# A four-layer graph network on one core: the second pair of squared edge components, read from memory instead of made by TensorE

## The chip, the core and the metric
The kernel runs on one core of a Trainium2 chip. The metric is the device time of one execution in microseconds. Five engines work on separate instruction streams and meet through semaphores: PE (TensorE, matmuls into the accumulator banks), DVE (VectorE), ACT (ScalarE), POOL (GpSimd) and SP (SyncE, which issues DMAs).

## The reference, cut to what matters
The reference runs four graph layers over 3125 nodes with 64 features and 103125 edges that are sorted by destination. The second layer is the one that the change touches. For each edge it forms, in the logits:

```python
h   = gelu(gelu(edge_attr_64 @ Wk1) @ Wk2)          # 64 hidden numbers of an edge
k   = f(h @ Wk3)                                    # times x[src], and times edge_sh (8 components)
q   = node_feat[edge_dst]
scal = concat([q * k0, einsum('ed,eds,es->ed', q, k1, edge_sh)])
edge_logit = scal @ W_logit                         # 4 heads
```

`k1` already holds one factor `edge_sh[s]`, so the sum over the eight components carries each component squared. The kernel therefore needs, for every edge, the product of a hidden number with the square of component s, for s = 0 to 7, before a matmul with the part of `Wk3` that belongs to s.

## The kernel before, in words
The first and the last two layers work on a dense count matrix and lie outside the change. Between them stand two edge passes over 202 tiles (`T`) of 512 edges (`TW`); the change is in the first, which makes the logits.

In the first pass edges lie along the free dimension of most tiles. Two components go into one 128-partition tile: component 2j on partitions 0 to 63 and 2j+1 on 64 to 127, each repeated over its 64 partitions. Pairs j = 0, 1 are the first pair of products (`bt_pair[0]`), j = 2, 3 the second (`bt_pair[1]`).

The squares are made for 16 tiles at a time (`CT`; 13 groups, `CN`): VectorE's `split_step` squares the raw components (L1697), and cuts each square into three bf16 parts, which SP stores as 24 rows to `sh_rows` (L533). For each tile SP loads these rows twice (`p1_components`, L569). TensorE's `tb(t, j)` (L925) is a matmul of a 0/1 selection matrix with these rows: it adds the three parts and repeats a component over 64 partitions, into banks 5 and 6. VectorE's `times(t, i)` (L1751) multiplies both banks by the hidden tile `h2k` into `bt_pair[i]`. As there are two banks only, the order is: `tb` 0 and 1, `times` 0, `tb` 2 and 3, `times` 1, and then `tb` 0 and 1 of the next tile. TensorE's `kmm` (L931) multiplies each result by its weights.

Every engine's order is written out by hand. One turn of TensorE's loop (L993) holds: the hidden layer of tile t+1 (L949), the first `tb` pair of t-1, the second hidden layer of t (L939, L940), `kmm` 2 and 3 of t-2, the logits of t-3 (L959), a fold every fourth tile (L968), the transposes of t (L975), the second `tb` pair of t-1, the node's own part of t-1 (`p1_half`, L983, which waits for the product of the tile before), and `kmm` 0 and 1 of t-1. One turn of VectorE (`p1`) holds: `times` 0 of t-1, one step of filling in destination rows (`fill`, L1738), the product of t-2 with its node features (L1762), a `fill`, `times` 1 of t-1, two `fill`, and `both` (L1745, source times destination features of t+1, which raises `u_ready`); in 9 of 16 turns a `split_step` follows.

SP's turn (`p1_turn`) issues the store of gathered rows (`xs_dump`, L573), waits for `u_ready` (L1745) and then issues the loads of placed rows (L565) and edge attributes (L562) two tiles ahead, the component rows of t (L569), and the store of the value hidden tile (`hs_dump`, L578). GpSimd gathers source rows, four indirect DMAs a tile (L734): the first waits for `xs_dump` of the tile two before and for `u_ready`, the second for a `times` 0, the third for a product, the fourth for a `times` 1.

Of the kernel before, what the change touches and what calls it, by code (L numbers as in the profile page):

```python
# [16 lines left out]
P = 128  # L17
N, D, E = 3125, 64, 103125
# [5 lines left out]
TW = K * P  # L24
S = 8
CT = P // S
CN = -(-T // CT)
# [16 lines left out]
COLS = 512  # L44
# [18 lines left out]
class Steps:  # L63
# [5 lines left out]
    def ran(self, ins):  # L69
        ins.then_inc(self.sem, 1)  # L70
        self.n += 1
# [23 lines left out]
def build(nc, x_in, src_in, dst_in, dst_before, dst_after, ea64, ea8, ew, w0, a0, gam, bet, wk1, wk2, wk3, wv1, wv2, wv3,  # L95
          wlog, wout, w2, a2s, a2d, b2, aw3, const, out):
    F32, BF16, F16, I32 = mybir.dt.float32, mybir.dt.bfloat16, mybir.dt.float16, mybir.dt.int32
    ALU, ACT, AX = mybir.AluOpType, mybir.ActivationFunctionType, mybir.AxisListType.X
# [10 lines left out]
    placed_v = placed[0:P * W, :].rearrange("(p c) f -> p (c f)", p=P)  # L109
    xs_dump = nc.dram_tensor("xs_dump", (P, W * D), F32).ap()  # L110
    sh_rows = nc.dram_tensor("sh_rows", (2, CN, 3 * S, CT * TW), BF16).ap()
    hs_dump = nc.dram_tensor("hs_dump", (T, D, TW), F32).ap()
    run_rows = nc.dram_tensor("run_rows", (P * W, D), F32).ap()
    carry_rows = nc.dram_tensor("carry_rows", (HROWS, D), F32).ap()
# [2 lines left out]
    with ExitStack() as ctx:  # L117
# [3 lines left out]
        def sem(name):  # L121
            return ctx.enter_context(nc.semaphore(name))
# [128 lines left out]
        def stage():  # L251
            c = Carve()
            c.at = stage_at
            return c

        cw = stage()
        wk3n, wv3n = cw(9 * D), cw(9 * D)
        eat = [cw(TW // 2) for _ in range(2)]
        sht = [cw(TW, BF16) for _ in range(2)]
        ut = [cw(TW // 2) for _ in range(2)]  # L260
        h1 = [cw(TW) for _ in range(2)]
        lgt = cw(P)
# [2 lines left out]
        bt_pair = [cw(2 * TW) for _ in range(2)]  # L265
# [6 lines left out]
        raw, square = ([cw(TW) for _ in range(2)] for _ in range(2))  # L272
# [29 lines left out]
        banks = ctx.enter_context(nc.psum_tensor("banks", [P, 8 * COLS], F32))  # L302
# [44 lines left out]
        hs_out = [sem(f"hs_out{i}") for i in range(2)]  # L347
        u_ready, ut_ps, ut_sb = sem("u_ready"), sem("ut_ps"), sem("ut_sb")
        sht_in = [sem(f"sht_in{i}") for i in range(2)]
        h1_ps, h1_sb, h2_ps, h2k_sb, h2v_sb = (  # L350
            sem("h1_ps"), sem("h1_sb"), sem("h2_ps"), sem("h2k_sb"), sem("h2v_sb"))
        tb_ps, bt_sb, half_k, yk_ps, prod_sb, lg_ps, lg_sb = (
            sem("tb_ps"), sem("bt_sb"), sem("half_k"), sem("yk_ps"), sem("prod_sb"), sem("lg_ps"), sem("lg_sb"))
# [25 lines left out]
        def at(sem_, value, eng):  # L379

            if not (isinstance(value, int) and value <= 0):
                eng.wait_ge(sem_, value)
# [29 lines left out]
        def _(sp):  # L412
# [51 lines left out]
            for i in range(SL // 8):  # L464
# [3 lines left out]
                if lo < W * D:  # L468
                    n = min(CROW, W * D - lo)
# [59 lines left out]
            def store_components(c):  # L529
                sp.wait_ge(split_sb, c + 1)  # L530
                for v in range(2):
                    for k in range(3):
                        sp.dma_start(sh_rows[v, c, k * S:(k + 1) * S, :].rearrange("s (g n) -> (s g) n", g=CT),  # L533
                                     parts[v][k][c % 2]).then_inc(split_out[c % 2], 16)

            def components_stored(c):
                sp.wait_ge(split_out[c % 2], 16 * 6 * (c // 2 + 1))

            sp.wait_ge(p_ready, NB)
            sp.wait_ge(agg_ps, 4)  # L540
# [3 lines left out]
            for k in range(2):  # L544
                r = slice(k * D, (k + 1) * D)
# [11 lines left out]
            for s_ in range(S):  # L557
                half = s_ % 2
# [8 lines left out]
            def p1_components(t, par):  # L567
                for k in range(2):
                    sp.dma_start(sht[par][D * k:D * k + 3 * S, :], sh_rows[0, t // CT, :, t % CT * TW:(t % CT + 1) * TW]).then_inc(sht_in[par], 16)  # L569

            def p1_rows(t, par, n):
                sp.wait_ge(gathered[par], n)
                sp.dma_start(xs_dump[:, bass.ds(t * (K * D), K * D)], xs[par]).then_inc(xs_out[par], 16)  # L573
# [7 lines left out]
            def p1_turn(t, par, n, more=True):  # L581
                p1_rows(t, par, n)
                if more:
                    sp.wait_ge(u_ready, t + 1)
                    p1_first(t + 2, par)
                    sp.wait_ge(h1_ps, t + 1)
                    p1_load(t + 2, par)
                if t > 1:
                    sp.wait_ge(tb_ps, t * 2 - 2)
                    p1_components(t, par)  # L590
                if t:
                    p1_value(t - 1, 1 - par)

# [1 line left out]
                p1_load(par, par)  # L595
            sp.wait_ge(h_ready, 4)
            sp.dma_start(h_table[0:NP, :].rearrange("(b p) f -> p b f", p=P), h[:, :, :]).then_inc(table_out, 16)
            store_components(0)
            components_stored(0)
            for par in range(2):  # L600
                p1_components(par, par)
            sp.wait_ge(placed_out, 16 * NB)
            for par in range(2):
                p1_first(par, par)
            for t in range(T):
                c = t // CT + 1
                if t % CT == CT - 3 and c < CN:
                    store_components(c)
                    if c + 1 < CN:
                        load_components(c + 1)  # L610
                if t % CT == 0 and t:
                    components_stored(c - 1)
                p1_turn(t, t % 2, (t // 2 + 1) * full, t + 2 < T)
# [183 lines left out]
        def _(pe):  # L797
# [118 lines left out]
            def p1_turned(t):  # L916

                pe.wait_ge(sht_in[t % 2], (t // 2 + 1) * 32)
                at(bt_sb, t * 2, pe)
                tb(t, 0)  # L920
                tb(t, 1).then_inc(tb_ps, 1)

            def tb(t, j):
                rows = slice(D * (j % 2), D * (j % 2 + 1))
                return pe.matmul(ps[5 + j % 2][:, :], sel[rows, j, :], sht[t % 2][rows, :], start=True, stop=True)  # L925
# [67 lines left out]
            for t in range(-1, T + 4):  # L993
                if edge(t + 1):
                    p1_hidden(t + 1)
                if edge(t - 1):
                    p1_turned(t - 1)
                if edge(t):
                    p1_second(t)
                if edge(t - 2):  # L1000
                    kmm(t - 2, 2)
                    kmm(t - 2, 3).then_inc(yk_ps, 1)
                if edge(t - 3):
                    p1_logits(t - 3)
                pe.wait_ge(h1_sb, min(t + 2, T))
                if group_done(t - 4):
                    p1_fold((t - 4) // 4)
                if edge(t):
                    p1_transpose(t)
                if edge(t - 1):  # L1010
                    pe.wait_ge(bt_sb, t * 2 - 1)
                    tb(t - 1, 2)
                    tb(t - 1, 3).then_inc(tb_ps, 1)
                    p1_half(t - 1)
            barrier(pe, 2)

# [367 lines left out]
        def _(dve):  # L1384
            st = Steps(dve, dve_steps)
            do, ran, settle = st.do, st.ran, st.settle
            V = nc.vector
# [291 lines left out]
            for part in range(2):  # L1679
                r = slice(*HALVES[part])  # L1680
                row = [P, r.stop - r.start, D]
# [9 lines left out]
            def split_step(c, i):  # L1691

                r = c % 2
                if i == 0:
                    dve.wait_ge(raw_in[r], 16 * (c // 2 + 1))
                    at(split_out[r], 16 * 6 * (c // 2), dve)
                    ran(V.tensor_tensor(square[r], raw[r], raw[r], ALU.mult))  # L1697
                    return
                v = (square if i < 5 else raw)[r]
                high, mid, low = (p[r] for p in parts[0 if i < 5 else 1])  # L1700
                settle()
                if i % 4 == 1:
                    ran(V.tensor_copy(out=high, in_=v))
                elif i % 4 == 2:
                    ran(V.tensor_tensor(v, v, high, ALU.subtract))
                elif i % 4 == 3:
                    ran(V.tensor_copy(out=mid, in_=v))
                elif i == 4:
                    ran(V.tensor_tensor(low, v, mid, ALU.subtract))
                else:  # L1710
                    V.tensor_tensor(low, v, mid, ALU.subtract).then_inc(split_sb, 1)
# [33 lines left out]
                V.tensor_tensor(u[par], xs[par], xd[par], ALU.mult).then_inc(u_ready, 1)  # L1745

            def times(t, i):
                dve.wait_ge(tb_ps, t * 2 + i + 1)
                dve.wait_ge(h2k_sb, t + 1)
                at(yk_ps if i else half_k, t, dve)  # L1750
                V.tensor_tensor(bt_pair[i].rearrange("p (j n) -> p j n", j=2), banks[:, 5 * COLS:7 * COLS].rearrange("p (j n) -> p j n", j=2),  # L1751
                                h2k[t % 2].rearrange("p (o n) -> p o n", o=1).to_broadcast([P, 2, TW]), ALU.mult).then_inc(bt_sb, 1)

            def product(t, par):
# [148 lines left out]
            for part in range(2):  # L1903
                r = slice(*HALVES[part])
# [10 lines left out]
            for k, layer in enumerate((2, 3)):  # L1915
# [16 lines left out]
                for j in range(NJ):  # L1932
                    n = min(4, NB - 4 * j)
# [9 lines left out]
                for j in range(NJ):  # L1943
                    n = min(COLS, NP - j * COLS)
# [26 lines left out]
                for part in range(2):  # L1971
                    r = slice(*HALVES[part])
# [12 lines left out]
            for part in range(2):  # L1985
                r = slice(*HALVES[part])
# [71 lines left out]
```

## Time and profile before
| | |
|---|---|
| time of three runs | 4709.61, 4718.47, 4720.08 us; median 4718.47 |
| the profiled execution | 4691.75 us, its span 4690.0 us |
| busy share of the span | PE 73%, DVE 80%, ACT 46%, POOL 40% |
| the first edge pass | 1180 to 2580 us of the span |
| the second edge pass | 2710 to 3990 us of the span |

The profile is one execution. Busy time counts an engine's instructions, not its waits, and not the instructions that only wait, branch or issue a DMA. "Idle before" is the time that an engine stood still ahead of an instruction, with the instruction or DMA whose semaphore ended it; "issue" means that it waited for nothing the trace shows, "remote" that the semaphore's update has no instruction close before it. PE's records give the time at which a matmul was sent into the array and a modelled end. One matmul of 32-bit numbers shows as two records.

### The profile page before, as it was taken

What the parts mean: (1) busy time and instruction counts of PE and PEld (TensorE: products, weight loads), DVE (VectorE), ACT (ScalarE), POOL (GpSimd) and SP (SyncE); (2) the same over time, 40 slices, a digit from 0 to 9 for tenths busy, and PEclk for the clock granted to TensorE, in tenths of its full rate; (3) what the DMA queues carried; (4) which work ended last, traced back from release to release, by engine and by line L of the source; (5) the groups of instructions that cost most, each with busy time, mean ns of one, the idle gap of its engine ahead of it and who ended that gap; (6) DMA issues with size and microseconds to landing.
All of it is one profiled execution on the core that took longest, in us unless ns stands there. A gap on an engine that the chain in (4) does not pass through costs nothing. (4 is left out here: it accounts for less than half of the span.)

```text
span 4690.0 us, 65792 instructions
## 1 busy us (share of the span) xinstructions
PE 3424.4 (73%) x20105; PEld 1508.5 (32%) x20105; DVE 3775.0 (80%) x6298; ACT 2138.1 (46%) x4386; POOL 1853.7 (40%) x3682
## 2 busy tenths in 40 slices
PE   5665653465688888888888089999999999248157
PEld 2111111111233343333333034444444444112122
DVE  8999995898566666666666878888888888599898
ACT  6999991674233333333333033444434443047066
POOL 0100445000655555555554056666666666200000
PEclk9989885677899999999999589999999999579589
DMA  4754999663344444444443023333333333356445
GB/s 174 303 223 162 313 326 317 219 210 113 99 120 116 113 115 113 115 113 112 117 114 104 4 78 94 91 93 93 91 94 91 93 93 88 127 176 227 158 177 184
DMA packets 373210, 675.89 MB, mean 144 GB/s; under 512 B 74684, under 2 KB 274940, under 8 KB 361216
## 3 DMA queue, kind: packets, MB, share of 16 engines
q1 hardware_dynamic: 308752, 569.80, 37.0%
q0 software_dynamic: 39568, 78.78, 6.8%
q10 hardware_dynamic: 24544, 23.10, 1.7%
q8 instruction: 167, 2.74, 0.3%
q14 instruction: 179, 1.47, 0.1%
HBM read 399.80 MB, written 271.65 MB: 143 GB/s over the span
## 5 line engine op out<-in xcount | busy, mean ns | idle before, releaser
L734 POOL DMA_INDIRECT arena<-h_table,srci x808 | 772.5, 956 | 596.3 <-issue 244.2
L1751 DVE TENSOR_TENSOR arena<-banks,arena 128x1024 f32<-128x1024 f32 x404 | 493.6, 1222 | 262.9 <-remote 162.9
L829 PE MATMUL banks<-arena 128*128 128x500 bf16 x1440 | 411.4, 416 | 273.9 <-DVE arena L1474 211.4
L1871 DVE TENSOR_TENSOR arena<-banks,arena 128x512 f32<-128x512 f32 x808 | 518.8, 684 | 36.5 <-PE banks L1036 13.0
L1879 DVE TENSOR_TENSOR arena<-banks,arena 128x512 f32<-128x512 f32 x808 | 516.9, 681 | 1.3 <-PE banks L1042 1.3
L1166 ACT ACTIVATE arena<-arena,h 128x128 bf16<-128x128 f16 x1440 | 465.1, 416 | 61.0 <-DVEq L1390 40.9
L1318 ACT ACTIVATE arena<-banks 64x256 f32<-64x256 f32 x808 | 306.3, 379 | 341.2 <-PE banks L1068 334.2
L931 PE MATMUL banks<-arena 128*64 128x256 f32 x3232 | 451.2, 402 | 0.0
L1056 PE MATMUL banks<-arena 128*64 128x256 f32 x3232 | 438.5, 392 | 0.5 <-DVE arena L1881 0.5
L1042 PE MATMUL banks<-arena 64*128 64x512 f32 x1616 | 436.2, 617 | 1.2 <-DVE arena L1879 0.9
L1462 DVE TENSOR_SCALAR arena<-arena,agg 128x500 bf16<-128x500 f16 x1440 | 413.3, 362 | 0.2
L759 POOL TENSOR_TENSOR arena<-arena,same_prev 128x64 f32<-128x64 f32 x808 | 237.4, 294 | 395.0 <-ACT arena L1328 347.5
L886 PE MATMUL banks<-arena,proj 128*65 128x512 f32 (+1 forms) x700 | 278.1, 549 | 89.4 <-DVE arena L1959 89.4
L1255 ACT ACTIVATE arena<-banks 128x512 f32<-128x512 f32 x202 | 120.7, 598 | 483.7 <-PE banks L949 263.3
L684 POOL DMA_INDIRECT arena<-slots,slot_i x157 | 173.2, 1103 | 356.4 <-DMA slots<-arena 316.0
L931 PEld LDWEIGHTS banks<-arena 128*64 128x64 f32 x3232 | 222.3, 142 | 261.0 <-issue 156.6
L829 PEld LDWEIGHTS banks<-arena 128*128 128x128 bf16 x1440 | 123.9, 102 | 560.4 <-DVE arena L1462 429.6
L760 POOL TENSOR_TENSOR arena<-arena 128x64 f32<-128x64 f32 x808 | 259.0, 321 | 63.4
L886 PE MATMUL banks<-arena,lw 128*64 128x512 f32 (+1 forms) x350 | 183.3, 688 | 134.7 <-DVE lw L1645 134.7
L1056 PEld LDWEIGHTS banks<-arena 128*64 128x64 f32 x3232 | 196.0, 136 | 246.1 <-DVE arena L1881 153.3
L1173 ACT ACTIVATE arena<-arena,ones 128x512 bf16<-128x512 bf16 x360 | 265.3, 737 | 12.7 <-PE banks L829 12.6
L1762 DVE TENSOR_TENSOR arena<-banks,arena 128x512 f32<-128x512 f32 x202 | 139.3, 689 | 163.0 <-remote 86.4
(296 smaller groups left out, 6422.5 us busy)
## 6 DMA issues: line engine op xcount, KB each, us to landing
arena<-c_flat SPq DMA_DIRECT2D x75, 1562.5 KB, 6.8
slots<-arena SPq DMA_DIRECT2D x90, 1000.0 KB, 3.8
arena<-hs_dump SPq DMA_DIRECT2D x404, 128.0 KB
arena<-mask_rows SPq DMA_DIRECT2D x50, 781.2 KB, 4.3
arena<-in_edge_attr SPq DMA_DIRECT2D x202, 128.0 KB
arena<-placed SPq DMA_DIRECT2D x202, 128.0 KB
xs_dump<-arena SPq DMA_DIRECT2D x202, 128.0 KB
hs_dump<-arena SPq DMA_DIRECT2D x202, 128.0 KB
```

Source lines behind the costliest of these rows:

```text
L734: pool.indirect_dma_start(out=xs[par][:, k * D:(k + 1) * D], out_offset=None, in_=h_table, in_offset=bass.IndirectOffsetOnAxis(ap=srci[:, ...
L829: last = pe.matmul(ps[4 + r % 2][:, 0:BW], row_hot[r][:, k * P:(k + 1) * P], col_hot[r][:, k * BW:(k + 1) * BW], start=k == 0, stop=k == K ...
L886: last = pe.matmul(ps[j][0:rows, 0:n], proj[:, b, 2:rows + 2] if base else lw[par][:, :], ptile[par][:, j * COLS:j * COLS + n], start=b == ...
L931: last = pe.matmul(ps[7][k * D:(k + 1) * D, 0:TW // 2], k3[j], bt[j][:, k * (TW // 2):(k + 1) * (TW // 2)], start=j == 0, stop=j == 3)
L1042: pe.matmul(ps[5 + j % 2][:, :], v3[j][rows, :], hv[t % 2][rows, :], start=True, stop=True).then_inc(y_ps, 1)
L1056: last = pe.matmul(ps[2][k * D:(k + 1) * D, 0:TW // 2], wo[j], vt[j][:, k * (TW // 2):(k + 1) * (TW // 2)], start=j == 0, stop=False)
L1166: last = act.activation(apart[r % 4][:, k * P:(k + 1) * P], iota16[:, 0:P], ACT.Abs, bias=minus_key[:, k, bass.ds(s, 1)])
L1318: copied = act.activation(xat[r][half * D:(half + 1) * D, k * (TW // 2):(k + 1) * (TW // 2)], ps[0][k * D:(k + 1) * D, 0:TW // 2], ACT.Copy)
L1462: made = V.tensor_scalar(col_hot[r][:, k * BW:(k + 1) * BW], iota16[:, 0:BW], col_key[:, k, bass.ds(s, 1)], None, ALU.is_equal)
L1751: V.tensor_tensor(bt_pair[i].rearrange("p (j n) -> p j n", j=2), banks[:, 5 * COLS:7 * COLS].rearrange("p (j n) -> p j n", j=2), h2k[t % 2 ...
L1871: V.tensor_tensor(dt_[j % 2], ps[3 + j % 2][:, :], xat[t % 3], ALU.mult).then_inc(dt_sb, 1)
L1879: V.tensor_tensor(vt[j], ps[5 + j % 2][:, :], dt_[j % 2], ALU.mult).then_inc(vt_sb, 1)
```

## The change
The upper four components' squares are stored as 32-bit rows (`sq_rows`) right after they are made. For each tile SP spreads four of these rows over 64 partitions each by a DMA that reads one row of 2 KB 64 times, into `sqt`. `times` 1 multiplies `sqt` by the hidden tile, and `tb` 2 and 3 are gone; the first `tb` pair waits for `times` 0 of the tile before. `tb_ps` now counts once a tile. The three bf16 parts of all eight squares are still made and loaded.

```diff
+    sq_rows = nc.dram_tensor("sq_rows", (CN, S // 2, CT * TW), F32).ap()
+        sqt = [cw(2 * TW) for _ in range(2)]
             def components_stored(c):
                 sp.wait_ge(split_out[c % 2], 16 * 6 * (c // 2 + 1))
+                sp.wait_ge(square_out[c % 2], 16 * (c // 2 + 1))
+            def store_squares(c):
+                sp.wait_ge(squared, c + 1)
+                sp.dma_start(sq_rows[c].rearrange("s (g n) -> (s g) n", g=CT), square[c % 2][P // 2:P, :]).then_inc(square_out[c % 2], 16)
+            def p1_spread(t, par):
+                for j in range(2):
+                    for half in range(2):
+                        row = sq_rows[t // CT, 2 * j + half, t % CT * TW:(t % CT + 1) * TW].rearrange("(o n) -> o n", o=1)
+                        sp.dma_start(sqt[par][half * D:(half + 1) * D, j * TW:(j + 1) * TW], row.to_broadcast([D, TW])).then_inc(sqt_in[par], 16)
                 if t > 1:
-                    sp.wait_ge(tb_ps, t * 2 - 2)
+                    sp.wait_ge(tb_ps, t - 1)
                     p1_components(t, par)
+                    sp.wait_ge(bt_sb, t * 2 - 2)
+                    p1_spread(t, par)
+            store_squares(0)
             store_components(0)
...
                 p1_components(par, par)
+                p1_spread(par, par)
...
+                if t % CT == 1 and c < CN:
+                    store_squares(c)
             def p1_turned(t):
                 pe.wait_ge(sht_in[t % 2], (t // 2 + 1) * 32)
-                at(bt_sb, t * 2, pe)
+                at(bt_sb, t * 2 - 1, pe)
                 if edge(t - 1):
-                    pe.wait_ge(bt_sb, t * 2 - 1)
-                    tb(t - 1, 2)
-                    tb(t - 1, 3).then_inc(tb_ps, 1)
                     p1_half(t - 1)
             def split_step(c, i):
-                    ran(V.tensor_tensor(square[r], raw[r], raw[r], ALU.mult))
+                    V.tensor_tensor(square[r], raw[r], raw[r], ALU.mult).then_inc(squared, 1)
                     return
+                if i == 1:
+                    dve.wait_ge(squared, c + 1)
+                if i == 2:
+                    dve.wait_ge(square_out[r], 16 * (c // 2 + 1))
             def times(t, i):
-                dve.wait_ge(tb_ps, t * 2 + i + 1)
+                if i:
+                    dve.wait_ge(sqt_in[t % 2], 16 * 4 * (t // 2 + 1))
+                else:
+                    dve.wait_ge(tb_ps, t + 1)
                 dve.wait_ge(h2k_sb, t + 1)
                 at(yk_ps if i else half_k, t, dve)
+                basis = sqt[t % 2] if i else banks[:, 5 * COLS:7 * COLS]
```

## Rows read from the trace of the kernel before
**Rows 1.** First pass: us; busy us (instructions) of PE, PEld, DVE, ACT, POOL; clock; DMA.
```profile
1180.00:2580.00 1400.00, 1160.46 (x8586) 542.06 (x8586) 939.18 (x1749) 431.81 (x910) 784.55 (x820) 0.93 0.42 113
```
**Rows 2.** Line L1255: count, duration ns min/median/max, first and last start.
```profile
L1255 ACT ACTIVATE arena<-banks x202: 597/598/602, 1188.2 to 2564.8; 128x512 f32<-128x512 f32 x101
```
**Rows 3.** Instructions of PE in order of time: start us, us, what.
```profile
1924.36 0.39 PE L925 MATMUL banks<-arena,sel 64*128 64x512 bf16 x2
1924.68 0.65 PE L983 MATMUL banks<-arena 128*64 128x256 f32 x4
...
1929.57 0.39 PE L925 MATMUL banks<-arena,sel 64*128 64x512 bf16 x2
1929.89 0.44 PE L983 MATMUL banks<-arena 128*64 128x256 f32 x2
```
**Rows 4.** Groups of DVE, 1500 to 2300: busy us, mean ns, idle before, releasers.
```profile
L1751 DVE TENSOR_TENSOR arena<-banks,arena 128x1024 f32<-128x1024 f32 x235 | 287.1, 1222 | 142.0 <-remote 83.8 <-PE banks L925 46.3 <-issue 9.3
L1762 DVE TENSOR_TENSOR arena<-banks,arena 128x512 f32<-128x512 f32 x118 | 81.4, 690 | 107.3 <-remote 63.1 <-PE banks L931 23.9 <-issue 19.6
L1705 DVE TENSOR_TENSOR arena<-arena 128x512 f32<-128x512 f32 x14 | 9.6, 689 | 0.0
```
**Rows 5.** Waits, 1500 to 2300: total us, times, longest us.
```profile
PE banks L983 <- DVE arena L1762: 65.9, 55, 4.5
POOL arena L734 <- DMA xs_dump<-arena: 21.3, 9, 5.5
PE banks L925 <- DVE arena L1751: 13.6, 23, 2.0
```
**Rows 6.** Instructions in order of time around one late activation.
```profile
1911.96 0.70 PE L949 MATMUL banks<-arena 64*128 64x256 f32 x4
...
1915.71 0.60 ACT L1255 ACTIVATE arena<-banks 128x512 f32<-128x512 f32 x1 [3.90 <-remote]
```
**Rows 7.** Line L629, loads of 64 x 2 KB in the second pass: issue ns.
```profile
L629 SPq DMA_DIRECT2D arena<-hs_dump x404: 450/450/976, 2708.2 to 3980.1; - x135
```
**Rows 8.** Issues of SP in order of time: the stores of a group, another turn.
```profile
1834.97 3.04 SPq L533 DMA_DIRECT2D sh_rows<-arena  x6
...
1927.02 0.34 SPq L565 DMA_DIRECT2D arena<-placed  x1
1927.41 0.43 SPq L562 DMA_DIRECT2D arena<-in_edge_attr  x1
1927.88 0.81 SPq L569 DMA_DIRECT2D arena<-sh_rows  x2
...
1929.22 0.59 SPq L573 DMA_DIRECT2D xs_dump<-arena  x1
```
**Rows 9.** Waits of SP, 1500 to 2300: total us, times, longest us.
```profile
SPq L565 <- DVE arena L1745: 364.0, 100, 5.4
```
**Rows 10.** Landings: L441's broadcasts, min/median/max us; a 128 KB load, median us.
```profile
DMA to landing us min/median/max: 2.8/2.8/2.9
...
arena<-xs_dump SPq DMA_DIRECT2D x202, 128.0 KB, 2.3
```
**Rows 11.** The first instruction of DVE after the splitting of the first group.
```profile
1197.53 0.38 DVE L1735 COPY arena<-seed 128x64 f32<-128x64 f32 x1 [12.04 <-DMA arena<-placed]
```
**Rows 12.** Scatters of POOL beside DVE, in order of time.
```profile
1168.41 0.89 DVE L1686 TENSOR_TENSOR h<-h,betb 128x704 f32<-128x704 f32 x1
1168.67 1.46 POOL L713 DMA_INDIRECT placed<-h,start_i  x1 [0.30 <-issue]
...
1170.44 0.96 POOL L713 DMA_INDIRECT placed<-h,start_i  x1 [0.30 <-issue]
```
**Rows 13.** A gather of POOL beside DVE, in order of time.
```profile
1899.76 0.42 DVE L1745 TENSOR_TENSOR arena<-arena 128x256 f32<-128x256 f32 x1
1899.87 1.14 POOL L734 DMA_INDIRECT arena<-h_table,srci  x1 [0.30 <-issue]
```
**Rows 14.** The gathers, 1500 to 2300: busy us, mean ns, idle before, releasers.
```profile
L734 POOL DMA_INDIRECT arena<-h_table,srci x471 | 450.2, 956 | 350.6 <-issue 137.0 <-DVE arena L1751 126.9 <-DVE arena L1762 65.0
```

More of the change, by code:

```diff
@@ L349, in build @@
         sht_in = [sem(f"sht_in{i}") for i in range(2)]
+        sqt_in = [sem(f"sqt_in{i}") for i in range(2)]
+        squared, square_out = sem("squared"), [sem(f"square_out{i}") for i in range(2)]
         h1_ps, h1_sb, h2_ps, h2k_sb, h2v_sb = (
@@ L1747, in times @@
             def times(t, i):
-                dve.wait_ge(tb_ps, t * 2 + i + 1)
+                if i:
+                    dve.wait_ge(sqt_in[t % 2], 16 * 4 * (t // 2 + 1))
+                else:
+                    dve.wait_ge(tb_ps, t + 1)
                 dve.wait_ge(h2k_sb, t + 1)
                 at(yk_ps if i else half_k, t, dve)
-                V.tensor_tensor(bt_pair[i].rearrange("p (j n) -> p j n", j=2), banks[:, 5 * COLS:7 * COLS].rearrange("p (j n) -> p j n", j=2),
+                basis = sqt[t % 2] if i else banks[:, 5 * COLS:7 * COLS]
+                V.tensor_tensor(bt_pair[i].rearrange("p (j n) -> p j n", j=2), basis.rearrange("p (j n) -> p j n", j=2),
                                 h2k[t % 2].rearrange("p (o n) -> p o n", o=1).to_broadcast([P, 2, TW]), ALU.mult).then_inc(bt_sb, 1)
```

## The prediction
> **What bounds the kernel now.** I began with the table of stretches. The first edge pass is the stretch from 1180 to 2580 us: 1400 us, VectorE busy for 939 of them, TensorE for 1160, TensorE's granted clock 0.93, the DMA engines busy for 0.42 of the time at 113 GB/s; no engine is full [rows 1]. The hidden-layer activation runs once a tile, 202 times, from 1188.2 to 2564.8 us [rows 2]: 6.85 us a tile.
>
> Next I read TensorE's instructions in order of time where it runs without gaps. There a tile takes from one second pair of selection matmuls (1924.36) to the next (1929.57), 5.21 us [rows 3]. A mean tile is therefore 1.64 us longer than TensorE's gapless one. The waits say where that goes. VectorE stands idle 142.0 us before its 235 basis products, 0.60 us each, 83.8 of it until something that the trace can't name ("remote") and 46.3 until the selection matmuls [rows 4]. TensorE waits 65.9 us, in 55 of some 118 tiles, before L983 for the product L1762, and 13.6 us before L925 for the basis product [rows 5].
>
> "Remote" has a pattern: TensorE's hidden matmuls L949 are over at 1912.66 by their records, yet the activation that waits for little else starts at 1915.71, after 3.90 us of idleness [rows 6]. TensorE's results reach the others some 3 us after its records end. I call this a hold-up; nothing in these rows tells its cause. So a tile's pace is TensorE's stream, plus hold-ups, plus handovers between TensorE and VectorE.
>
> **The change, part by part.**
>
> *TensorE loses a pair of matmuls.* From the second pair's start to the next instruction's start 0.32 us pass, at 1924.36 and again at 1929.57 [rows 3]. 202 tiles x 0.32 = -65 us. Bounds: -65, and 0 where TensorE would only wait longer for L1762 behind it. I take -65, since the gapless stretch shows TensorE setting the pace.
>
> *The second basis product no longer waits for that pair.* If half the idleness of rows 4 belongs to the second product and all of it goes: 0.60 x 202 = -121 us; 0 if it moves on to the next wait. An earlier VectorE helps only where TensorE later waits for it, 55 of 118 tiles [rows 5], and only for the part that isn't "remote", 58.2 of 142.0 us [rows 4]: 121 x 0.47 x 0.41 = -23 us, which I take.
>
> *The first pair waits for the first product of the tile before, not the second.* At most the 13.6 us of rows 5, over 118 tiles: 0.115 x 202 = -23. The second pair shares in that number, and L983 follows soon; I take half, -12.
>
> *The second product reads memory on both sides.* 128x512 with one side in PSUM (L1762) takes 690 ns, with both in memory (L1705) 689 ns [rows 4]. Twice as wide, the change is 2 ns at most either way: 0.
>
> *SP issues four more DMAs a tile.* A 64 x 2 KB load holds SP for 0.45 us (L629) [rows 7]; with the gaps of 0.04 to 0.05 us between SP's issues [rows 8], 2.0 us a tile. Its two new waits are for events that precede the one SP has just waited for (u_ready comes after the second product of the same turn), so they cost nothing. SP waits 364.0 us for the end of VectorE's turn, 3.1 us a tile over 118 [rows 9]: this cover hides the 2.0 us. It is gone once in 16 tiles, where six stores take 3.04 us and a load follows [rows 8]: about 2.4 us late, 12 times, 29 us if nothing hid it. SP issues loads two tiles ahead, so I take +5.
>
> Behind the four new DMAs stand the two stores hs_dump and xs_dump. A gather two tiles later waits for xs_dump, which now does so in 9 tiles, 21.3 us together [rows 5].
>
> *The rows spread over partitions.* 512 KB more a tile is 77 GB/s beside 113, and at the ratio of rows 1 (0.42 for 113) a DMA share of 0.71. The engines have room. 64 partitions read one row of 2 KB; the near case in the trace is a broadcast of 256 B to 128 partitions, landed 2.8 us after issue, where a plain 128 KB load lands after 2.3 [rows 10]. Needed over a tile later, it is hidden at either value. If the four came one after another, each with such a landing of 2.8 us, a tile would need 11.2 us; I don't believe this, but no row excludes it.
>
> *The squares' store at the start* delays VectorE's splitting by a landing, 2.3 to 2.8 us [rows 10]; VectorE then idles 12.04 us for the placed rows [rows 11]. Nothing. In the twelve later groups the store has a whole tile: nothing.
>
> *GpSimd's gathers.* A scatter that starts inside a VectorE instruction with two operands in memory (1168.67, inside L1686) takes 1.46 us where the next takes 0.96 [rows 12], and a gather that starts 0.11 us into L1745 takes 1.14 instead of the mean 0.956 [rows 13, 14]. The second product becomes such an instruction, 1.22 us long, so a gather that starts in it may lose up to 1.1 us: 0 to +222 us if one did in every tile and all of it told. GpSimd's idleness beyond its 0.30 us between gathers is 350.6 - 471 x 0.30 = 209 us, 1.8 us a tile [rows 14], and one gather of each tile is released only by the end of the second product. I take +20, a tenth of a microsecond a tile, for gathers that start late and then pack closer.
>
> The Trainium skill speaks against the change here (SBUF — State Buffer, "Who interferes with whom"): a VectorE instruction with two SBUF inputs excludes a GpSimd instruction that reads SBUF for its whole length, and one with a single SBUF input doesn't. Rows 12 and 13 agree in kind: 0.50 and 0.19 us were lost. By the rule alone, a held gather in every tile would be 1.22 x 202 = 246 us of GpSimd's time, still within its idleness above.
>
> **Sum.** -65 - 23 - 12 + 5 + 20 = -75 us. The profiled execution took 4691.75 us (span 4690.0), so 4617 by it; it lies 26.7 us below the median of the three runs, 4718.47, and against that the forecast is 4643 us.
>
> **The rivals.**
>
> A, *the gather queue becomes the bound* (slower). Four gathers at 0.956 us and 0.30 us between them are 5.0 us a tile [rows 13, 14]. Add 1.1 us for one held in the second product, and up to 2.0 us for an xs_dump issued behind the four new DMAs. It decides once the loss passes 6.85 - 5.0 = 1.85 us a tile. With 1.1 and 1.1 (half of the dump's delay, some of it being slack) a tile takes 7.2: +0.35 x 202 = +71, 4789 us. For: the lengthened gathers, and the tight dump in 9 tiles. Against: 1.8 us of slack, and a gather is issued a tile or more before its use.
>
> B, *the hold-ups swallow it*. They take 1.64 us a tile, more than everything freed; where VectorE stands "remote", TensorE's saved slot ends in the same wait. Then the time is 4718, give or take 15. For: 83.8 of the 142.0 us. Against: the time between hold-ups is TensorE's own.
>
> C, *the whole wait goes*: -65 - 121 - 23 = -209, 4509 us. Against: L983 still waits for L1762, which needs the last matmuls of the same turn.
>
> D, *the rows come late* because all partitions read one place: a tile would take at least the 11.2 us of four broadcasts landing in turn, +4.35 x 202 = +880 us.
>
> **How the numbers follow.** Forecast 0.38, A 0.26, B 0.22, C 0.10, D 0.04. The forecast's own range is 4600 to 4690. 4560 to 4800 leaves out C, D and the worst of A, 2 in 10. No change is within 0.2%, 9.4 us, which is what a measurement of this kernel can tell. Faster: 0.35 of the forecast's, C's 0.10 and 0.07 of B's, 0.52. Same: 0.03 and 0.10, 0.13. Slower: A, D and 0.05 of B, 0.35.
>
> **What would show it.** Right: the selection matmuls at 404 instead of 808 in the pass; VectorE's idleness before the second product near zero, before the first and before L1762 longer; SP's wait for L1745 near 1.1 us a tile; DMA share near 0.7; a tile of 6.5 us. A would show as gathers of 1.2 us and more in the mean and as waits of L1745 for them. B as an unchanged tile with more "remote". D as VectorE waiting before the second product for the DMA of the spread rows. The forecast is wrong if a tile isn't between 6.25 and 6.7 us, or if the second product takes more than 1.25 us.

## The result, and the profile after

The changed kernel takes 4773.86 us (median of four runs, 4765.66 to 4776.94) where the kernel before takes 4715.66 (four runs, 4709.61 to 4720.08): 1.0122 of before, with a 95% interval of 1.0103 to 1.0140. I had forecast 4643 us. The other runs below were made in groups on different chips, each beside its own runs of the kernel before, whose medians lie between 4686 and 4716 us. So ratios are compared rather than times; 1% is 47 us.

All of the loss is in the first edge pass. In the traces of all runs but one_spread (below), what lies outside that pass (between the first and the last start of u's product) takes 3314 to 3324 us, so most of the 30 us between the medians lies in the first pass too. A ratio is therefore a safe measure only within one group; where two groups are compared below, the times and the traced passes stand beside it. The same view of it as in [rows 1], the pass being longer now, and the activation of [rows 2]:

```profile
1180.00:2660.00 1480.00, 1133.02 (x8110) 542.51 (x8110) 926.30 (x1748) 430.52 (x906) 891.52 (x818) 0.89 0.65 178
...
L1273 ACT ACTIVATE arena<-banks x202: 597/597/600, 1190.5 to 2653.4; 128x512 f32<-128x512 f32 x101
```

A tile takes (2653.4 - 1190.5) / 201 = 7.28 us instead of 6.85, where 6.5 was forecast; the pass is 86 us longer from the first of these activations to the last, the whole profiled execution 85 us. TensorE's granted clock is 0.89 where it was 0.93, and GpSimd is busy for 107 us more in about as many gathers. VectorE's groups, to be held against [rows 4]:

```profile
L1777 DVE TENSOR_TENSOR arena<-arena 128x1024 f32<-128x1024 f32 x111 | 135.3, 1219 | 1.1 <-issue 1.0
L1777 DVE TENSOR_TENSOR arena<-banks,arena 128x1024 f32<-128x1024 f32 x110 | 134.5, 1223 | 175.5 <-PE banks L946 83.4 <-remote 76.3 <-issue 15.5
L1788 DVE TENSOR_TENSOR arena<-banks,arena 128x512 f32<-128x512 f32 x110 | 75.9, 690 | 83.2 <-PE banks L952 34.8 <-remote 29.3 <-issue 17.5
```

The second product (from memory, 1219 ns beside 1223 from the banks) no longer waits. The first one alone now waits 175.5 us, more than the 142.0 of both before; the wait ahead of L1788 fell (83.2, where L1762 had 107.3), against the sign that I had given. Where the waits went shows in SP. Its issues in order of time, one whole turn between two stores of xs_dump (columns as in [rows 8]), then the spread's line (as in [rows 7]) and SP's waits (as in [rows 9]):

```profile
1908.29 0.59 SPq L588 DMA_DIRECT2D xs_dump<-arena  x1
1908.93 0.44 SPq L574 DMA_DIRECT2D arena<-placed  x1
1909.41 0.47 SPq L571 DMA_DIRECT2D arena<-in_edge_attr  x1
1909.92 0.81 SPq L578 DMA_DIRECT2D arena<-sh_rows  x2
1910.78 2.37 SPq L584 DMA_DIRECT2D arena<-sq_rows  x4
1913.19 0.59 SPq L593 DMA_DIRECT2D hs_dump<-arena  x1
1913.83 0.59 SPq L588 DMA_DIRECT2D xs_dump<-arena  x1
```

```profile
L584 SPq DMA_DIRECT2D arena<-sq_rows x440: 101/596/1501, 1503.6 to 2299.2; - x147
```

```profile
SPq L574 <- DVE arena L1767: 95.6, 35, 8.2
SPq L546 <- DVE arena L1715: 25.7, 7, 6.7
```

A turn of SP without any wait is 1913.83 - 1908.29 = 5.54 us: longer than TensorE's gapless tile before, 5.21 us [rows 3]. SP waits for VectorE's turn to end in 35 of 110 turns; before, it was in 100 of 118. What it issues is late, and others wait for it (columns as in [rows 5]; before, the gathers' wait was 21.3 us):

```profile
POOL arena L755 <- DMA xs_dump<-arena: 87.1, 52, 3.9
...
ACT arena L1283 <- DMA hs_dump<-arena: 26.6, 18, 2.6
...
PEld banks L970 <- DMA arena<-in_edge_attr: 22.6, 18, 2.0
```

VectorE in turn waits 19.0 us for gathers that are late, before L1767.

And the gathers, as in [rows 14], have grown from 956 to 1090 ns:

```profile
L755 POOL DMA_INDIRECT arena<-h_table,srci x440 | 479.6, 1090 | 322.0 <-issue 109.1 <-DMA xs_dump<-arena 87.1 <-DVE arena L1777 75.0
```

Three suspects follow: SP's issues (theory 1), the two-operand product that holds the gathers (theory 2), the bytes of the spreads (theory 3). A fourth question is where the gain on TensorE went.

### The profile page after: what moved, and what is told of

Read it like the earlier page. It is cut to its first block and busy times, and to the rows that moved or that the text cites. A ratio compares the mean times of both kernels' runs of the same rounds, so it can differ in the third digit from the quotient of the medians.

```text
span 4774.7 us, 65831 instructions
## 1 busy us (share of the span) xinstructions
PE 3402.8 (71%) x19701; PEld 1511.3 (32%) x19701; DVE 3764.6 (79%) x6298; ACT 2135.4 (45%) x4386; POOL 1968.6 (41%) x3682
## 5 line engine op out<-in xcount | busy, mean ns | idle before, releaser
L755 POOL DMA_INDIRECT arena<-h_table,srci x808 | 882.6, 1092 | 579.9 <-issue 204.9
L1897 DVE TENSOR_TENSOR arena<-banks,arena 128x512 f32<-128x512 f32 x808 | 518.6, 683 | 36.8 <-PE banks L1054 13.1
L1905 DVE TENSOR_TENSOR arena<-banks,arena 128x512 f32<-128x512 f32 x808 | 516.7, 681 | 0.4 <-PE banks L1060 0.4
L1777 DVE TENSOR_TENSOR arena<-banks,arena 128x1024 f32<-128x1024 f32 x202 | 247.0, 1223 | 331.2 <-remote 163.1
L1184 ACT ACTIVATE arena<-arena,h 128x128 bf16<-128x128 f16 x1440 | 454.3, 386 | 59.1 <-DVEq L1408 40.1
L952 PE MATMUL banks<-arena 128*64 128x256 f32 x3232 | 464.6, 412 | 0.3 <-DVE arena L1777 0.3
L1074 PE MATMUL banks<-arena 128*64 128x256 f32 x3232 | 437.9, 392 | 0.5 <-DVE arena L1907 0.5
L970 PE MATMUL banks<-arena 64*128 64x256 f32 x808 | 166.5, 492 | 185.8 <-issue 118.2
L1328 ACT ACTIVATE arena<-banks 128x256 f32<-128x256 f32 x202 | 77.4, 383 | 421.5 <-PE banks L1076 421.5
```

Of the source, the lines that this page charges most:

```text
L755: pool.indirect_dma_start(out=xs[par][:, k * D:(k + 1) * D], out_offset=None, in_=h_table, in_offset=bass.IndirectOffsetOnAxis(ap=srci[:, ...
L952: last = pe.matmul(ps[7][k * D:(k + 1) * D, 0:TW // 2], k3[j], bt[j][:, k * (TW // 2):(k + 1) * (TW // 2)], start=j == 0, stop=j == 3)
L1074: last = pe.matmul(ps[2][k * D:(k + 1) * D, 0:TW // 2], wo[j], vt[j][:, k * (TW // 2):(k + 1) * (TW // 2)], start=j == 0, stop=False)
L1184: last = act.activation(apart[r % 4][:, k * P:(k + 1) * P], iota16[:, 0:P], ACT.Abs, bias=minus_key[:, k, bass.ds(s, 1)])
L1897: V.tensor_tensor(dt_[j % 2], ps[3 + j % 2][:, :], xat[t % 3], ALU.mult).then_inc(dt_sb, 1)
L1905: V.tensor_tensor(vt[j], ps[5 + j % 2][:, :], dt_[j % 2], ALU.mult).then_inc(vt_sb, 1)
```

## Experiments: what the spreads cost

**two_dma.** One spread for each half of the partitions (in this cut VectorE's count of them is left out, and "..." stands for text):

```
-                for j in range(2):
-                    for half in range(2):
-                        row = sq_rows[t // CT, 2 * j + half, ...]
-                        sp.dma_start(sqt[par][half * D:(half + 1) * D, j * TW:(j + 1) * TW], row.to_broadcast([D, TW]))
+                for half in range(2):
+                    rows = sq_rows[t // CT, half::2, ...].rearrange("(o j) n -> o j n", o=1)
+                    sp.dma_start(sqt[par][half * D:(half + 1) * D, :]..., rows.to_broadcast([D, 2, TW]))
```

> The kernel after, but a tile's rows come by two spreads, one for each half of the partitions with both its rows, instead of four: the same bytes, two issues of SyncE fewer, about 1.2 us a tile by the 596 ns of one. Theory 1 (SyncE's queue has become the bound: its free time fell from 364.0 to 95.6 us over 110 tiles): the time falls from 4774 to 4690 +- 25, and the waits for late stores (gathers behind the node store 87 us, TensorE behind the edge load 14 to 23 us) mostly go. Theory 2 (the product that reads two operands from SBUF holds the gathers up) and theory 3 (the spreads' bytes crowd the other transfers): 4774 +- 8.

Measured: 1.0059 (1.0040 to 1.0078). Half of the loss went with half of the issues, the bytes being the same (few_bytes, below, has all four issues in the same group and stands at 1.0126). On the scale of the expectation that is 4743 us, between its two ranges; and the gathers' wait for xs_dump, which theory 1 wanted mostly gone, is 102.5 us where it was 87.1.

**few_bytes.** `sqt[par][half * D:(half + 1) * D, j * TW:j * TW + TW // 16]`: a sixteenth of the bytes in four issues.

> The kernel after with the same four spreads a tile, but each brings only 32 of a row's 512 columns (the rest of the operand stays zero, so that the second pair's products are left out for those columns). Theory 1 (issues): 4774 +- 10, since SyncE issues as much as before. Theory 3 (bytes): the first pass loses what the crowding costs, 4640 to 4690, with gathers that land earlier and DMA's share back from 0.66 to about 0.43.

Measured: 1.0126 (1.0097 to 1.0156). The DMA engines' share is back at 0.44 and the time is not: theory 3 falls. One issue takes SP 596 ns in the median, as with all the bytes.

**no_spread.** The four spreads and VectorE's wait for them are gone.

> The kernel after without the four spreads and the wait for them (the second pair's operand stays zero); the squares' store and its waits stay, and the second product still reads two operands from SBUF. Theories 1 and 3: the cost was the spreads, so the gain of TensorE's pair appears, 4640 +- 30. Theory 2 (the lock of the product): 4750 to 4775, with gathers that still take about 1.09 us each.

Measured: 1.0002 (0.9993 to 1.0012). The 1.2% belongs to the spreads, but no theory had foreseen that nothing would be gained without them.

**late_squares.** `if t % CT == 2` instead of `== 1` ahead of the squares' store.

> The kernel after with the squares' store of a group of 16 tiles issued one turn of SyncE later, when VectorE has made the squares. Theory 1 in its narrow form (SyncE stands 25.7 us in 7 group turns of 800 us, 44 us over the first pass, and what is behind it is late): 4735 +- 15. If that wait only takes time that SyncE would spend in the next wait: 4774 +- 8.

Measured: 1.0106 (1.0081 to 1.0131); alone it can't be told from 1.0122.

**four_fewer.** SP keeps the four spreads and loses four other issues (the waits and counts that go with them are left out here):

```
-                    p1_load(t + 2, par)
...
-                    p1_components(t, par)
...
-                if t:
+                if 0 < t < 3:
                     p1_value(t - 1, 1 - par)
```

> The kernel after with its four spreads, but four other issues of SyncE a tile left out: the edge attributes and the two loads of components are brought for the first two tiles alone and used for all, and the hidden rows are stored for two tiles (the second pass reads those two in turn; values left out). SyncE's issues take 5.39 us of a tile after, 2.86 before. Theory 1 (the sum of SyncE's issues sets the loss, whichever they are): 0.998 to 1.004 of before, as with no spread. Rival (the spreads' own transfers or their waits set it): 1.009 to 1.014.

Measured: 1.0037 (1.0022 to 1.0053). Most of the loss goes although the spreads stay; the centre is at the upper end of what theory 1 gave, and the squares' store is still in its place (SP waits 34.0 us for the squares, 25.7 in after). Summed over the first pass, SP's issues take 2.72 us a tile in no_spread, 3.28 in four_fewer, 4.25 in two_dma and 5.39 in after; the ratios rise in the same order.

**one_spread.** The rows are laid out so that a single DMA, `rows.to_broadcast([2, D, 2 * TW])`, fills all 128 partitions.

> The kernel after with the rows laid out in memory so that one spread brings a tile's four rows to 128 partitions: the same bytes, three issues of SyncE fewer (two stores of squares a group instead of one). Theory 1, in proportion to the issues (no spread 1.0002, two 1.0059, four 1.0122 of before): 1.003 +- 0.002. If the price is one of having spreads at all: 1.005 or more.

Measured: 1.2425 (1.2402 to 1.2447). The expectation missed by far: this DMA itself is slow. VectorE waits for it in every tile, and in after hardly ever (waits, 1500 to 2300 us):

```profile
DVE arena L1776 <- DMA arena<-sq_rows: 325.1, 65, 5.7
```

SP is held as well: the issue of the hs_dump store right behind the spread takes 5.88 us in the median, in after 0.60. 512 KB came in one DMA whose outermost dimension is 2, where the other spreads have 64. The Trainium skill (DMA: Bandwidth & Descriptors, "Rules for kernel authors") says that an outermost dimension under 16 confines a DMA to at most that many engines, here two. The runs agree as far as they go: the DMA share fell to 0.33 while the transfer was waited for; which engines it used was not read.

**two_dma_late.** The whole computation, two_dma and late_squares together.

> The whole computation, as after, with two spreads a tile in place of four and the store of squares one turn later. If the parts add up (1.0059 less 0.0016): 1.002 to 1.007, slower than before still, since with no spread at all it is 1.0002. A version that beats before by 0.2%: under 0.998.

Measured: 1.0020 (1.0011 to 1.0030). It is the best form of this change that I found, and it doesn't beat the kernel before. By the ratios the later store is worth 0.4%, 18 us; but two_dma was in another group, and by the times this kernel is the slower one (4726 beside 4718 us). So what the later store is worth is not shown.

## Experiments: where TensorE's gain went

**lock_only.** The kernel before, TensorE's second pair still made, with `basis = sqt[t % 2] if i else banks[...]` for the product.

> The kernel before, with TensorE's second pair still made and waited for, whose second product reads an operand of zeros in SBUF (the second pair's products are left out). Theory 2: the lock costs what no_spread lost, 40 to 70 us over before (1.009 to 1.015), gathers at 1.09 us. Rival: within 10 us of before (0.998 to 1.002) although gathers take 1.09 us.

Measured: 0.9994 (0.9982 to 1.0007). Gathers take 1034 ns, where after has 1090, and the pass the same time: theory 2 falls for the kernel before. Together with the spreads it was not tried by itself.

**psum_pair.** no_spread with `basis = banks[:, 5 * COLS:7 * COLS]` for both products and `at(bt_sb, t * 2, pe)` ahead of the first pair.

> The kernel after without spreads, whose second product reads the first pair's banks in place of the operand in SBUF (it takes the first pair's values, and TensorE's next first pair waits for both products as before the change). Against no_spread (1.0002 of before) it differs by the two-SBUF product alone. Theory 2 (the lock ate the gain): 50 to 75 us under before, 0.984 to 0.989, gathers back at 0.96 us. Rival (late semaphore updates of TensorE and its lower clock eat the gain whatever the product reads): within 10 us of no_spread, 0.998 to 1.002.

Measured: 1.0112 (1.0069 to 1.0155). It has less work than the kernel before, no lock, and SP's old load but for the squares' store, and is slower, outside both of the expected ranges. So I tried its wait by itself.

**late_first.** no_spread with `at(bt_sb, t * 2, pe)`.

> no_spread (1.0002 of before) with one wait put back: TensorE's first pair waits for both products of the tile before instead of the first alone. psum_pair (1.0112) has that wait too and reads the banks. If this wait is what parts the two: 1.008 to 1.014. If the operand in SBUF does it, by moving the gathers apart: 0.998 to 1.004.

Measured: 1.0008 (0.9995 to 1.0020). Only the operand parts it from psum_pair, and the one with the longer gathers is the faster, by the times too (4716.74 beside 4748.51 us, the groups being different; gathers of psum_pair, then of late_first):

```profile
L749 POOL DMA_INDIRECT arena<-h_table,srci x445 | 423.7, 952 | 378.2 <-DVE arena L1769 135.7 <-issue 116.5 <-DVE arena L1780 84.4
```
```profile
L749 POOL DMA_INDIRECT arena<-h_table,srci x466 | 517.3, 1110 | 284.8 <-issue 112.4 <-DVE arena L1769 93.7 <-DMA xs_dump<-arena 29.3
```

This pointed to the gathers. Before that, the trace of no_spread shows that TensorE did get shorter. Its stream without gaps, from one selection pair to the next:

```profile
2104.06 0.38 PE L940 MATMUL banks<-arena,sel 64*128 64x512 bf16 x2
...
2109.09 0.38 PE L940 MATMUL banks<-arena,sel 64*128 64x512 bf16 x2
```

5.03 us against the 5.21 of [rows 3]. Of the 201 tiles between two starts of u's product on VectorE, 74 are now under 5.5 us (21 before), but 50 are over 8 us (21 before), and the mean is 6.76 after 6.80. More tiles are short and more are long. Over these tiles TensorE is busy for 5.50 us of a tile, after 5.70, and idle for 1.27, after 1.10: what the pair freed comes back as idleness.

**plain_before, plain_nospread, plain_after.** In each of the three kernels the gather by list is replaced:

```
-                    pool.indirect_dma_start(out=xs[par][:, k * D:(k + 1) * D], out_offset=None, in_=h_table, in_offset=...)
+                    pool.dma_start(xs[par][:, k * D:(k + 1) * D], h_table[0:P, :])
```

> The kernel before with each gather by a list of rows replaced by a plain transfer of 128 rows in order on GpSimd's queue (every edge takes the same rows: values left out). If the late updates of TensorE's semaphores (83.8 us of VectorE's waits in 800 us) come from the gathers' making of addresses: these waits fall under 20 us and the time by 60 to 140 us. If not, the time falls by at most 30 us and the late updates stay.

> no_spread with plain transfers in place of the gathers by list (values left out), to be held against plain_before (0.9369 of before, 4389 us, tile 5.21 us, no late updates of TensorE). Theory 5 (the gain of TensorE's pair is there in undisturbed tiles, and the late updates that come with the gathers swallow it): tile 5.03 us, 36 us under plain_before, 0.927 to 0.931. Rival (the pair's removal gives nothing in any tile): 0.935 to 0.939.

> The kernel after with plain transfers in place of the gathers by list (values left out). SyncE's issues take 5.39 us of a tile plus the gaps between them, so without late updates theory 1 has SyncE as the bound: a tile of 5.7 to 6.2 us, 80 to 180 us over plain_nospread, 0.945 to 0.968 of before. Rival (SyncE does not bound): within 15 us of plain_nospread.

Measured: 0.9369 (0.9352 to 0.9386), 0.9251 (0.9231 to 0.9270), 0.9662 (0.9642 to 0.9682). The first is twice the largest fall that I had expected (300 us, not 60 to 140). Without lists no wait ends with "remote" in any of the three, and without lists and spreads the tile is nearly the gapless one (line of u's product on VectorE, plain_before and plain_nospread; columns as in [rows 2]):

```profile
L1744 DVE TENSOR_TENSOR arena<-arena x202: 424/425/427, 1194.5 to 2264.7; 128x256 f32<-128x256 f32 x101
```
```profile
L1760 DVE TENSOR_TENSOR arena<-arena x202: 424/425/427, 1198.6 to 2243.6; 128x256 f32<-128x256 f32 x101
```

5.32 and 5.20 us a tile in the mean, 5.21 and 5.03 in the median one. Here the pair's removal pays: 25 us in the traced passes (1070.2 and 1045.0 us from the first start to the last), 27 us in the times (4388.70 and 4361.76), where 36 were expected. The ratios would say 1.2%, 55 us, but the two come from different groups, whose kernels before lie 24 us apart; the plain kernels' tiles don't show that difference, since theirs are TensorE's gapless ones. And here SP bounds by itself: its issues take 5.56 us of a tile of 6.11, and the gaps of 0.04 to 0.05 us between ten of them most of the rest. In plain_after it waits for VectorE's turn in 8 of 130 turns, and the gathers wait for xs_dump in each (1500 to 2300 us):

```profile
SPq L574 <- DVE arena L1766: 8.0, 8, 2.0
```
```profile
POOL arena L755 <- DMA xs_dump<-arena: 500.6, 130, 8.3
```

The spreads cost 0.9662 - 0.9251 = 4.1% (one group; 193 us, a little over the 80 to 180 expected) where nothing else holds the pass.

**half_lists, three_lists, three_nospread.** Two, then three of a tile's four gathers by list, in the kernel before; three in no_spread (`if k % 2:` or `if k:` ahead of the indirect form, the plain form otherwise).

> The kernel before with two of a tile's four gathers by list, the others plain transfers of 128 rows in order (values left out). If the late updates go with the number of lists: midway between before and plain_before (0.9369), 0.96 to 0.975, and about half the late updates. If they come only when lists follow each other closely: 0.937 to 0.952. If one list a tile is enough for them: over 0.985.

> The kernel before with three of a tile's four gathers by list, the first a plain transfer (values left out). If lists are served one after another in some 1.7 us each (6.8 us a tile over four), three take 5.1 us and hide in TensorE's 5.21: 0.932 to 0.945. If the loss grows with each list beyond two: 0.96 to 0.98.

> no_spread (1.0002 of before) with the same three lists and one plain transfer a tile. If TensorE sets the pace again with three lists: 0.8 to 1.3% under three_lists. If the lists still set it: within 0.3% of three_lists.

Measured: 0.9323 (0.9307 to 0.9339), 0.9518 (0.9501 to 0.9535), 0.9439 (0.9415 to 0.9464). Two lists cost next to nothing, less than any of my three expectations: 10 us by the times, 4398.72 beside the 4388.70 of plain_before. The third costs 62 us by the times (and in the traced passes; the ratios, of different groups, say 2%), its ratio lying between my two expectations, and the fourth 4.8%, 226 us, within one group. No wait ends with "remote" with two lists; it comes back with the third (VectorE's group as in [rows 4]; three_lists):

```profile
L1754 DVE TENSOR_TENSOR arena<-banks,arena 128x1024 f32<-128x1024 f32 x285 | 348.6, 1223 | 119.0 <-PE banks L928 82.2 <-remote 26.4 <-issue 8.1
```

With three lists the pair's removal gives 0.8% (0.9439 beside 0.9518, one group; 34 us), with none 27 us, with four nothing.

**nogates_before, nogates_psum.** The kernel before, and psum_pair, without the three waits between a tile's gathers (`at(bt_sb, t * 2 - 5, pool)` and its two fellows).

> The kernel before without the three waits that hold a tile's second, third and fourth gather back until VectorE's products of earlier tiles are done, so that the four follow each other. Theory 6 (gathers close together make TensorE's late updates longer, and that sets the pass): 1.004 to 1.03 of before. Rival (the start of the gathers is indifferent): 0.997 to 1.003.

> psum_pair (1.0112 of before) without the same three waits. Theory 6, for the part of these waits in psum_pair's loss (products end earlier, so they let the gathers go at worse places): the time moves by over 0.5% from psum_pair, to either side. Rival (the loss has nothing to do with where these waits let gathers go): 1.007 to 1.015.

Measured: 1.0507 (1.0485 to 1.0528), more than expected, and 1.0340 (1.0296 to 1.0384). With gathers that follow each other, VectorE's "remote" before its products rises from 83.8 to 197.0 us in nogates_before:

```profile
L1745 DVE TENSOR_TENSOR arena<-banks,arena 128x1024 f32<-128x1024 f32 x196 | 239.6, 1223 | 284.5 <-remote 197.0 <-PE banks L919 77.5 <-issue 9.7
```

psum_pair's edit is worth -1.7% without these waits (1.0340 beside 1.0507) and +1.1% with them: whether the gathers are held apart decides even the sign.

## Why the prediction was wrong, point by point

Forecast and measured time lie 133 us apart (-75 and +58 us). Two steps failed: 51 of the 133 are SP's, the rest is the gain that didn't come.

*SP's step*: "this cover hides the 2.0 us", +5 us. Between no spread and four the runs put 1.2%, 56 us. One issue takes 596 ns, not 450, but the size is the smaller part of the error. The cover was a mean over uneven tiles, 3.1 us a tile. In a gapless tile SP had 5.21 us [rows 3] and now needs 5.54, so in short tiles it falls behind, and what it brings is late in the next ones. That SP's issues cost the 1.2% is shown by two_dma, few_bytes, no_spread and four_fewer; that they do it through the short tiles is argued from the turn and from plain_after. My expectation of its wait, near 1.1 us a tile, came out almost right (95.6 us over 110 tiles, 0.9), and it was the wrong test. The Trainium skill (Perfetto Trace Analysis, "What "DMA-bound" means") names an issuing engine whose track is solid with DMAs as a bound of its own; the turn above and plain_after agree. Its advice there is larger descriptors. Their size made no difference here: few_bytes, with a sixteenth of the bytes in each, lost as much, and two_dma lost half with rows of the same 2 KB in half as many DMAs.

*TensorE's pair, VectorE's wait, the earlier first pair*, -65, -23 and -12, the larger miss: no_spread has all three, and where these terms and the +20 for the gathers make -80 us, it stands at 1.0002, +1 us. The step that failed is "I take -65, since the gapless stretch shows TensorE setting the pace": it sets the pace of the short tiles, not of the mean one. The pair does leave TensorE (5.21 to 5.03 us, 0.18, where I had taken 0.32 from the distance to the next start), and VectorE's second product does go without waiting. Without lists, it gives 27 us. With four lists a tile it is given back as idleness in more of the long tiles. This part went as my rival B said; its reason, that the saved slot ends in the same late update, fits the added idleness, but is not shown by itself (see the last paragraph).

*In the later groups the store has a whole tile: nothing.* Wrong. SP comes to the store a turn before VectorE makes the squares and stands 25.7 us in 7 groups. What mending it is worth is not shown (late_squares, two_dma_late).

*The second product from memory costs nothing*: right, 1219 and 1223 ns. *The rows arrive in time*: right, rival D didn't come; only in one_spread did VectorE wait for these rows in every tile (from 1500 to 2300 us 3.0 us in two_dma, and 20.2 in plain_after, where SP is the bound).

*GpSimd's gathers*, +20: they did lengthen, 956 to 1090 ns, by the rule that I had cited (the Trainium skill, SBUF — State Buffer, "Who interferes with whom"), and the traces agree with it (952 ns in psum_pair, 1110 in late_first, which differ by the operand alone). But the time didn't follow: 0.9994 in lock_only. As a price in the sum the rule was worth zero there.

*The rivals.* The time came out near A's 4789, but that is chance. A's dump behind four DMAs is there (87.1 us), and of its signs the waits of L1767 for gathers (19.0 us); its gathers of 1.2 us are not (1.09). But the wait for the dump isn't the price: it is 102.5 us in two_dma, at half the loss, and 52.8 in few_bytes, at the whole one. A's other half, the held gathers, cost nothing in lock_only. What happened is B for the gain, and on top of it an SP that I had called covered.

*Not settled*: by which mechanism gathers by list delay TensorE's updates, and why psum_pair loses where late_first doesn't. The "remote" waits of VectorE and ScalarE don't add up to the times: from 1500 to 2300 us they are 325 us before, 342 in no_spread, 382 in lock_only, which is as fast, and 295 in psum_pair, which is slower. TensorE's lower granted clock (0.94 before, 0.92 in no_spread, 0.90 in psum_pair, from 1500 to 2300 us) goes with the loss; whether as cause or as effect was not tried. Of the 1.48 us that part a tile of before (6.80) from one of plain_before (5.32, clock 1.00), 0.44 are longer busy time of TensorE (5.70 and 5.26 us) and the rest is its idleness. Issuing the spreads from another engine's queue, the direct way to relieve SP, was not tried either. late_first, no_spread and lock_only multiply zeros in the second pair; few_bytes, zeros for the most part, took the time of after, so I don't read the values as the cause.

## What to carry to other kernels

Read a queue's slack in the stage's gapless tile, not as its mean wait: sum the issues of one turn, add the new ones, and compare with the shortest tile. Work taken from an engine pays only if that engine still sets the pace when the stage is disturbed, so see first whether the mean tile or only the shortest one follows its stream. Count DMAs, not bytes, where the issuing engine is the limit; but a DMA merged over a short outermost dimension can cost far more than the issues it saves, as one_spread did. And compare two variants by their ratios only if both ratios rest on the same runs of the kernel before.

## What the runs showed of the hardware

Gathers by list cost this pass far more than GpSimd's time shows. Four a tile, at 0.956 us each, cost 6.3% of the whole kernel against plain transfers of as many rows (the same 128 each time; 0.535 us each), although the gathers keep GpSimd busy for only 56% of the time. What goes with them is found at another engine: the updates that VectorE and ScalarE wait for come late ("remote"; none without lists), and TensorE's granted clock is 0.94, not 1.00. Two a tile cost 10 us, four 300. A product that made the gathers longer left the kernel as fast (lock_only) or faster (late_first beside psum_pair).

An issue of SP took 596 ns in the median for 64 rows of 2 KB (after) and for 64 of 128 B (few_bytes), and 607 ns for twice as many rows of 2 KB (two_dma): in these runs the price is one of the DMA, not of its bytes.
